# Copies of value halves between the slots of packed context blocks: from VectorE to ScalarE

## What is computed

```python
# layer 0, cross attention: 8 heads of 64, keys and values from the context
kv_input = jnp.concatenate([x, latents], axis=1)     # 77 context rows, 128 tokens
k, v = jnp.split(kv_input @ Wkv, 2, axis=-1)         # q = latents @ Wq
q = l2norm(q) * q_scale
k = l2norm(k) * k_scale
sim = jnp.einsum('bhid,bhjd->bhij', q, k) * SCALE
attn = jax.nn.softmax(where(full_mask, sim, max_neg))
out = jnp.einsum('bhij,bhjd->bhid', attn, v)
...
x = x + xattn0(ctx, layernorm(x))      # the part above, then Wo and a layer norm
x = x + quantised_ffn(layernorm(x))    # int8 matmul
x = x + xattn1(layernorm(x), ctx)      # softmax(x We ctx^T) ctx, then W2
x = x + top1_of_8_experts(layernorm(x))
```

## Time and profile before

| | |
|---|---|
| three timed runs | 951.93, 954.2 and 954.86 us, median 954.2 |
| the profiled execution, first to last instruction | 950.6 us; the timed runs are 1.3 to 4.3 us above it |
| PE, PEld | busy 912.8 us (96%), 794.5 us (84%) |
| DVE, ACT, POOL | busy 744.9 us (78%), 693.5 us (73%), 458.1 us (48%) |
| the chain that ended last | PE 69%, DVE 14%, ACT 8%, issue 3%, POOL 3% |
| TensorE's granted clock, mean | 0.997 of full |

### The profile page before, as it was taken

One profiled execution on the slowest core, in us unless ns is written; L12 is line 12 of the kernel. 1 busy time (PEld: TensorE's weight loads), 2 busy tenths in 40 slices (PEclk: granted clock), 3 DMA queues, 4 the chain that ended last, 5 costly groups with the idle time before them and its releaser, 6 DMA issues.

```text
span 950.6 us, 30821 instructions
## 1 busy us (share of the span) xinstructions
PE 912.8 (96%) x11286; PEld 794.5 (84%) x11286; DVE 744.9 (78%) x2526; ACT 693.5 (73%) x1671; POOL 458.1 (48%) x1094
## 2 busy tenths in 40 slices
PE   7999999999999999999999999999999999899997
PEld 6788888788878887888788878888888878898997
DVE  5566787888888888888888888888888978877553
ACT  4877777677778787778777777777778766676664
POOL 5422433354535453545354444444454545777554
PEclk9999999999999999999999999999999999999999
DMA  7743000000000000000000000000000022245310
GB/s 196 200 124 57 2 2 2 2 13 2 14 2 14 2 14 2 13 3 10 5 10 5 8 8 8 7 8 7 8 8 8 7 47 71 61 97 106 95 55 20
DMA packets 45193, 31.44 MB, mean 33 GB/s; under 512 B 11555, under 2 KB 40166, under 8 KB 45046
## 3 DMA queue, kind: packets, MB, share of 16 engines
q1 hardware_dynamic: 39398, 19.93, 9.2%
q0 software_dynamic: 4320, 8.50, 2.8%
q10 hardware_dynamic: 1328, 1.06, 0.4%
HBM read 17.75 MB, written 12.17 MB: 31 GB/s over the span
## 4 chain that ended last, share of the span: by engine, by line
PE 69%; DVE 14%; ACT 8%; issue 3%; POOL 3%; DMA 1%; SPq 1%; DVEq 0%; POOLq 0%; ACTq 0%
PE ps L1670 9%; PE ps L1717 9%; PE ps L1643 7%; PE ps L1765 6%; PE ps L1450 5%; PE ps L1622 5%; PE ps L1630 5%; PE ps L1452 5%; PE ps L1451 5%; DVE sumsq L1267 4%; PE ps L1722 3%; ACT probs L604 2%; PE ps L1749 2%; ACT qk_hat L617 2%; PE ps L1496 1%
## 5 line engine op out<-in xcount | busy, mean ns | idle before, releaser
L1374 DVE TENSOR_TENSOR qk_hat<-ps,rstd 128x512 f32<-128x512 f32 x168 | 106.3, 684 | 49.2 <-POOL rstd L870 49.1
L1267 DVE TENSOR_REDUCE sumsq<-qk_hat 128x8 f32<-128x512 f32 x168 | 107.8, 677 | 35.9 <-ACT qk_hat L617 34.7
L863 POOL TENSOR_TENSOR rs_t<-rs_y 128x32 f32<-128x32 f32 x73 | 17.9, 245 | 235.2 <-ACT rs_y L658 235.2
L1670 PE MATMUL ps<-v_x,prob 128*64 128x65 f32 x2048 | 127.9, 225 | 2.1 <-ACT w_all L568 0.4
L1670 PE MATMUL ps<-v_c,prob 128*64 128x65 f32 x2048 | 124.2, 222 | 0.0
L677 ACT ACTIVATE prob<-ps,neg_shift 128x512 f32<-128x512 f32 x128 | 88.4, 690 | 48.6 <-PE ps L1717 48.6
L1670 PEld LDWEIGHTS ps<-v_x,prob 128*64 128x64 f32 x2048 | 105.0, 137 | 20.9 <-issue 19.2
L617 ACT ACTIVATE qk_hat<-ps 128x512 f32<-128x512 f32 x168 | 98.5, 599 | 31.7 <-PE ps L1452 25.8
L1450 PE MATMUL ps<-w_hi,xc_hi 128*128 128x512 f32 x272 | 120.8, 444 | 0.8 <-POOL xc_lo L835 0.8
L1717 PE MATMUL ps<-qT_all,kT_all 64*128 64x128 f32 x1536 | 111.6, 285 | 2.3 <-ACT prob L677 1.1
L1452 PE MATMUL ps<-w_hi,xc_lo 128*128 128x512 f32 x272 | 107.3, 395 | 0.0
(11 more groups left out here) (245 smaller groups left out, 2257.2 us busy)
## 6 DMA issues: line engine op xcount, KB each, us to landing
x_res<-sorted_rows SPq DMA_DIRECT2D x71, 65.5 KB, 1.9
w_all<-in_L_ffn_W_dram SPq DMA_DIRECT2D x16, 256.0 KB, 5.3
sorted_rows<-fill SPq DMA_DIRECT2D x8, 327.5 KB
out_dram<-prob,x_res POOLq DMA_INDIRECT x71
sorted_rows<-stage,idx POOLq DMA_INDIRECT x64, 2.4
ctx_res<-in_ctx_dram SPq DMA_DIRECT2D x8, 115.5 KB
x_res<-in_x_dram SPq DMA_DIRECT2D x1, 768.0 KB
sorted_rows<-fill SPq DMA_DIRECT2D x1, 524.0 KB, 5.0
```

Source lines behind the costliest of these rows:

```text
L1267: nc.vector.reduce_sum(sumsq[:, n * H:(n + 1) * H], sq[:, n * INNER:(n + 1) * INNER].rearrange("p (h d) -> p h d", d=DH), AX).then_inc(ss_ ...
L1374: nc.vector.tensor_tensor(qk_hat[:, n * INNER:(n + 1) * INNER].rearrange("p (h d) -> p h d", d=DH), ps_qk[:, n, :].rearrange("p (h d) -> p ...
L1670: last = nc.tensor.matmul(dst[half:half + DH, :], prob[:, kt, col + half:col + half + DH], v, start=kt == 0, stop=kt == 1)
```

## The change

ScalarE's `run` gets a helper `moves(some)` that issues the copies which VectorE issued before. The first copy of a fresh block stands ahead of `roots()`; the second, where there is one (p = 1 and 4), stands behind the last exponentials of the round, ahead of the next round's `qT_all`. VectorE's loop at the end of a fresh round is gone. The copies read and write the same rows and signal the same semaphore.

```diff
--- before.py
+++ after.py
@@ -699,6 +699,18 @@
 
                 if not inside and j == -1:
                     first_weights((0,))
+
+                def moves(some):
+
+                    if has(j, inside) and fresh(pos):
+                        block = FRESH[pos % LAP]
+                        act.wait_ge(v_copied, 2 * j + 2)
+                        for half, p in MOVES[block][some]:
+                            rows = slice(half * DH, (half + 1) * DH)
+                            nc.scalar.activation(v_c[rows, p % 4, :, 0:DH], v_c[rows, HOME[block] % 4, :, 0:DH],
+                                                 ACT.Copy).then_inc(v_moved, 1)
+
+                moves(slice(0, 1))
                 roots()
                 if tail(j, inside):
                     if has(j - 1, inside):
@@ -716,6 +728,7 @@
                     outputs_copied()
                 if has(j, inside):
                     exps((1, 3, 2))
+                moves(slice(1, None))
                 if not inside and j == -1:
                     first_weights((4, 5))
 
@@ -1394,13 +1407,6 @@
                                                    ALU.mult, ALU.add).then_inc(x1_done, 1)
                 if not tail(j, inside):
                     send(j, rho, g, inside)
-                if has(j, inside) and fresh(pos):
-
-                    block = FRESH[pos % LAP]
-                    dve.wait_ge(v_copied, 2 * j + 2)
-                    for half, p in MOVES[block]:
-                        rows = slice(half * DH, (half + 1) * DH)
-                        nc.vector.tensor_copy(v_c[rows, p % 4, :, 0:DH], v_c[rows, HOME[block] % 4, :, 0:DH]).then_inc(v_moved, 1)
                 if tail(j, inside):
                     finish(tile_no(j, 2))
                 if not inside and j == TAIL - 1:
```

## The result

The changed kernel took 957.23 us (median of 5 runs, 956.29 to 958.0) against 953.3 us of the kernel before (5 runs, 951.93 to 954.86): ratio 1.0041, 95% interval 1.0029 to 1.0053. Timed again in experiment e6 it was 955.69 against 953.15 us, ratio 1.0026, interval 1.0016 to 1.0035. It is slower by some 0.3%; I had forecast 1.0 us more (0.1%) and the measured is 2.5 to 3.9 us more.

A forecast was written before the change was run, and what follows sets the result against it. TensorE, busy 912.8 of 950.6 us, was taken as the bound, so only its waits count. Losses of 3.2 (p = 3) and 2.9 (p = 2) less 5.1 gained give + 1.0: 954.2 becomes 955.2 us, range 951.5 to 958.8.

The forecast's parts named there:

- the two cases that I gave 0.63 and 0.25: Whole kernel: time within 0.3% of before (chance 0.63), or slower by over 0.3%, above 957.1 us (chance 0.25).
- What VectorE gives back: At p = 5, TensorE's wait for o_c at line 1539 goes: 6 x 0.80 + 0.3 = 5.1 us gained.
- First copies covered at p = 0, 1, 4 and 6: Ahead of the roots, ScalarE's idle wait for var_in hides these copies, so they cost nothing.
- p = 3: No cover ahead of the roots; TensorE's second scores come 0.46 us later in seven rounds, 3.2 us lost.
- p = 2: Copy behind p = 1's exponentials delays lg_t; TensorE's line 1516 loses 0.49 us in six rounds, 2.9 us.
- I take 0.50: Assumed microseconds a copy takes in ScalarE's queue, from o_t's 0.49; bounds 0.41 and 0.69.
- Begins two groups late: rounds 18, 26, ...: Layer 2's routing, served by lg_t, limits the p = 2 loss to rounds 18, 26, 34, 42, 50 and 58.
- I count nothing: First lap: no v_s, lg_t or line 1539 to wait at, so no gain or loss was counted.
- Rival 1: Stalls only change places and p = 5 gives nothing back: 954.2 + 6.1 = 960.3 us; chance in full 0.13.
- half-way case: Stalls of p = 2 and p = 3 each add a 0.1 to 0.25 us restart; chance 0.15 together with Rival 3.
- Rival 2: Losses at lines 1516 and 1722 vanish or are absorbed, leaving only the gain: 949.1 us; chance 0.12.
- Rival 3: Cover ahead of the roots fails, copies cost 0.69 us or more: 957.7 us; chance 0.15 together with half-way case.

The follow-up runs named there:

- e3: Kernel before with only the two copies of p = 4 moved to ScalarE, the others left on VectorE: 972.38 against 975.79 us, ratio 0.997.
- e7: Changed kernel with the second copy of p = 4 back on VectorE: p = 5 took 11.64 us; 958.5 us, one run.
- e8: Changed kernel with VectorE making all its copies as before and ScalarE repeating them into an unread spare tile: 962.6 us, one run.
- e1: Changed kernel with both copies of a block ahead of the roots, none behind the exponentials: 972.86 us, one run, against 975.79 for the kernel before.
- e10: Changed kernel with the copy of p = 3 made twice, first into a spare tile: p = 3 took 13.90 us; 985.63 us, one run.
- e2: Changed kernel with the two copies of p = 1 and p = 4 in the other order, row 64 first: p = 2 11.52 us; 976.42 us, one run.
- e4: Changed kernel with all ScalarE copies ahead of the roots, except p = 3's behind the exponentials: 972.45 against 975.79 us for the kernel before, ratio 0.997.

## Why the prediction was right, and where it was not

The forecast of 955.2 us and no clear change was near: 2.7 us more by the rounds and 2.5 us in the second timing, against 1.0 forecast. Both timings' intervals lie around the 0.3% bound, so the truth is at the edge between the two cases that I gave 0.63 and 0.25. Luck has a small part in it. The two large misses, 1.0 us for what a copy costs at p = 2 and 0.4 us for round 10, went the same way; of what I had not counted, 0.5 us more in the first lap and 0.6 us less behind the loop happen to cancel. By its steps:

- **What VectorE gives back: right.** 5.1 us forecast, 5.14, 5.08 and 5.19 measured (the changed kernel, e6, e3). The seventh wait, of round 61, was worth 0.46 us in place of 0.3. The start of the statistics at 0.27 us behind the round's start, the length of 1.82 against 0.98 us as the price of the wait, and the worthlessness of the other four rounds all held (e3, e7, e8), but for 0.2 us once, in round 7 of the first lap: it is that much shorter in every kernel in which VectorE has no copy at p = 6, and not in e3 and e8.
- **First copies covered at p = 0, 1, 4 and 6: right.** These rounds changed by 0.03 us at most. At p = 1 and 4 even two copies are covered (e1).
- **p = 3: right.** 3.2 us forecast (0.46 a round), 3.33 measured (0.48). The copy takes 0.52 us of the queue there and not 0.50 (e10). The 56 copies themselves took 0.626 us in the median. The Trainium skill (VectorE: DVE Perf Modes, The TRN2 errata) has 224 + 512 cycles at 1.2 GHz for a copy like this one, 0.613 us by my estimate, and the trace is 2% above it.
- **p = 2: the term was mis-sized.** The mechanism is the one given (TensorE's 1522 waits for `lg_t`, six times, and the loss goes with the copy's place in e1), but 2.9 us were forecast and 4.34 measured: 0.65 us in each of the six rounds in place of 0.49, and round 10 besides. The step that failed is "I take 0.50": the copy behind the exponentials starts at row 64, overlaps neither neighbour, and puts `lg_t` off by 0.73 us. The room, taken at 0.01 us, was about 0.10, since line 1522 started 0.05 us behind the end of `lg_t` and not 0.14; that took a part of the miss back. e2 halved the loss by exchanging the two copies.
- **"Begins two groups late: rounds 18, 26, ..." missed one.** Round 10, without `lg_t`, lost 0.43 us too. There TensorE goes from the values straight to the queries' product, and that product waited 0.47 us for `qT_all`:

```profile
135.08 0.63 ACT L710 ACTIVATE v_c<-v_c 64x512 f32<-64x512 f32 x1
135.74 0.69 ACT L576 ACTIVATE qT_all<-ps,scale_col 128x512 f32<-128x512 f32 x1
...
136.57 0.47 PE L1456 MATMUL ps<-w_hi,xc_hi 128*128 128x512 f32 x1 [0.47 <-ACT qT_all L576]
```

- **The first lap, where "I count nothing": not quite.** Round 2 took 0.26 us more and round 5 0.42 us more. Both are gone (to 0.02 us) in e1 and e4, where nothing stands behind the exponentials of p = 1 and 4, and round 5's is gone in e7, so they belong to the second copies. In round 5 line 1456 waited for `qT_all` as in round 10: the copy behind p = 4 is free only where line 1545 stands ahead of the queries' product, as it does from round 13 on.
- **The second copy behind p = 4, covered by 1.39 us ahead of the squares: right from the second lap on.** The squares' idle time there fell to 0.30 us and the round is as short as with VectorE relieved alone.
- **Rival 1** did not happen; of its half-way case (956 to 958.5 us) the size came in the first timing, by another cause. **Rival 2** did not: no stall was absorbed. **Rival 3** named a copy of 0.69 us at all places; it was 0.52 for a start at row 0, and for one at row 64 0.65, or 0.73 at `lg_t` with the lost overlap ahead of it.

What stays open: why the first timing had 1.3 us more than the rounds, and the start 1 to 2 us more in the profiles of the changed kernel, e7 and e8. The start varies by over 1 us in one and the same kernel, so I take it for no part of the change, but that was argued and not shown. Round 2's 0.26 us came without a wait that the profile shows, and the 0.6 us less behind the loop were not followed up.

## What to carry to other kernels

Where one engine is 96% busy and two others take turns in feeding it, do not count the moved microseconds: find for each moved instruction the next thing that the busy engine waits for, and what room it has there; three such places (p = 2, 3 and 5) made up the whole result here. A move can be right for one of the places and wrong for the others, so place them one by one: moved only to where ScalarE was idle ahead of a late input, and behind p = 3 to where TensorE had room for the delay, the same copies made the kernel faster (ratio 0.9931 and 0.997) instead of slower. An instruction put in front of a queue that runs without gaps puts off all behind it by its whole distance to the next, and costs this, less the reader's room, as soon as the busy engine reads one of them, even where the queue's engine is 27% idle over the whole kernel.

## What the runs showed of the hardware

A ScalarE copy of 64 rows of 512 numbers from SBUF to SBUF took 0.62 to 0.64 us whichever rows they were. Starting at row 0, between instructions that start at row 0, it began 0.10 to 0.16 us before the one ahead of it ended, and the next started 0.52 us after it, where that waited for nothing else. Starting at row 64 it began 0.02 to 0.03 us after the end of the one ahead, and the next started 0.64 to 0.66 us after it at the earliest. That held behind p = 1 and behind p = 4 in the changed kernel, for the start at p = 0 too, with other slots written (e4, e8), and in e2 it went with the half and not with the place. In e1 and e4, where a copy that starts at row 0 has one that starts at row 64 right behind it, the second started 0.65 us after the first and not 0.52. I had expected no difference. Whether it is the change of the start row between neighbours or row 64 in itself was not tried: no two neighbours here both start at row 64.
